# A decoder layer on one core: the expert gating moved into the last attention iteration

## The reference

```python
x = layernorm(x + self_attention(x))          # attends over the 8 entries, rotary by position, 16 heads of 16
x = layernorm(x + cross_attention(x, ctx))    # 375 context rows per entry, 16 heads of 64, gated by tanh
x = layernorm(x + moe(x))
# moe: logits = x @ gate_w (8 experts); the two largest are kept, softmax over the two;
#      sum over the chosen experts of w_e * swiglu(x, w1_e, w2_e, w3_e), hidden width 512,
#      plus a shared swiglu for every token
```

## Time and profile before

| | us |
|---|---|
| median of 3 runs | 819.84 (818.64 to 822.49) |
| the profiled execution | 820.82 |
| its span, first to last instruction | 819.0 |
| PE busy | 658.7 (80%) |
| DVE busy | 540.1 (66%) |
| ACT busy | 411.2 (50%) |
| POOL busy | 218.4 (27%) |

### The profile page before, as it was taken

The page is one execution under the profiler, slowest core; times in us unless marked ns, Lnnn a source line. Parts: engine busy times, 40 slices in busy tenths (PEclk is TensorE's granted clock), DMA queues, the critical chain, the costliest instruction groups (busy, mean ns, idle before and its releaser), DMA issues. The chain is left out here.

```text
span 819.0 us, 13429 instructions
## 1 busy us (share of the span) xinstructions
PE 658.7 (80%) x4168; PEld 527.8 (64%) x4168; DVE 540.1 (66%) x1124; ACT 411.2 (50%) x1021; POOL 218.4 (27%) x223
## 2 busy tenths in 40 slices
PE   5717679899899899889889889988767864789980
PEld 4616468678678687777778777867565452456650
DVE  3974366886886886887786877786747851963332
ACT  2314175584574565476465557554533621853431
POOL 3540031232231222232232133122212530233331
PEclk9865689999998998999998999999956986999995
DMA  9113200200110210210210110040216444533324
GB/s 285 46 40 120 62 1 11 78 26 13 53 49 0 61 51 0 61 51 0 51 61 0 37 50 26 11 128 28 78 52 217 139 143 138 174 60 58 53 33 102
DMA packets 55634, 54.24 MB, mean 66 GB/s; under 512 B 17256, under 2 KB 44976, under 8 KB 55600
## 3 DMA queue, kind: packets, MB, share of 16 engines
q1 hardware_dynamic: 51504, 48.61, 19.7%
q0 software_dynamic: 4096, 5.19, 3.9%
HBM read 43.67 MB, written 10.13 MB: 66 GB/s over the span
## 5 line engine op out<-in xcount | busy, mean ns | idle before, releaser
L582 POOL TENSOR_TENSOR probs<-probs,c_rcp 112x750 f32<-112x750 f32 x64 | 92.0, 1437 | 317.5 <-DVE c_rcp L942 317.5
L705 ACT ACTIVATE probs<-ps_s,c_neg 112x375 f32<-112x375 f32 x128 | 72.3, 575 | 30.3 <-DVE c_neg L934 30.1
L1243 PE MATMUL ps_t<-ident,probs 112*125 112x112 f32 x384 | 56.4, 285 | 21.3 <-DVE cpt_lo L946 21.2
L1243 PEld LDWEIGHTS ps_t<-ident,probs 112*125 112x125 f32 x384 | 50.0, 195 | 29.0 <-issue 24.4
L1543 POOL DMA_INDIRECT moe_sum<-gsh_hi,xs_in x21 | 33.6, 1602 | 106.4 <-DMA moe_sum<-gsh_hi,xs_in 63.6
L932 DVE TENSOR_REDUCE c_max<-ps_s 112x2 f32<-112x750 f32 x64 | 59.8, 934 | 2.2 <-PE ps_s L133 1.3
L613 ACT ACTIVATE kt_hi<-ps_o 128x376 fp32r<-128x376 f32 x64 | 31.4, 491 | 58.3 <-PE ps_o L133 58.3
L131 PE MATMUL ps_o<-cpt_hi,v_lo 125*128 125x224 f32 x192 | 58.1, 303 | 2.0 <-DVE kt_lo L821 1.7
L1863 PE MATMUL ps_h<-w_ex,xst_hi 128*128 (+1 forms) x168 | 58.2, 389 | 1.4 <-DVE xst_lo L1630 0.9
L946 DVE TENSOR_TENSOR cpt_lo<-ps_t,cpt_hi 125x672 fp32r<-125x672 f32 x64 | 54.6, 853 | 6.0 <-ACT cpt_hi L613 5.9
L131 PE MATMUL ps_o<-ctxt_hi,w_k_lo 128*128 128x376 f32 x128 | 49.9, 390 | 10.2 <-DVE oct_lo L821 10.0
(11 more groups left out here) (289 smaller groups left out, 1946.4 us busy)
## 6 DMA issues: line engine op xcount, KB each, us to landing
chunk<-in_L_ffn_ew_dram SPq DMA_DIRECT2D x24, 512.0 KB, 3.5
spare<-in_L_ffn_ew_dram SPq DMA_DIRECT2D x18, 512.0 KB
store<-in_L_ffn_ew_dram SPq DMA_DIRECT2D x6, 512.0 KB, 5.8
ctx_raw<-in_ctx_dram SPq DMA_DIRECT2D x8, 375.0 KB
moe_in<-chunk SPq DMA_DIRECT2D x1, 2709.0 KB, 14.8
xs_in<-moe_in SPq DMA_DIRECT2D x21, 129.0 KB
plain_raw<-in_L_xattn_w_kv_dram SPq DMA_DIRECT2D x2, 1024.0 KB, 15.0
store<-in_L_ffn_sw_dram SPq DMA_DIRECT2D x3, 512.0 KB, 6.5
```

What stands on the lines that cost most here:

```text
L582: pool.tensor_tensor(p, p, r, ALU.mult).then_inc(sg["p_normed"], 1)
L705: act.activation(probs[:, s % 2, h, :], ps_s[0:N, h, 0:SK], ACT.Exp, bias=c_neg[:, s % 2, h:h + 1], scale=CROSS_SCALE, accum_out=c_sum[:, ...
L1243: last = pe.transpose(ps_t[0:SKT, h, t * N:(t + 1) * N], probs[:, s % 2, h, t * SKT:(t + 1) * SKT], ident[0:N, 0:N])
```

## The change

Nothing of what is computed changes but the order in which overflow tiles are given out. The edits:

- **Places in the last iteration.** A function `late` on each engine. PE's entries are in the table `LATE_PE`, which gives (pair, place) to step; on DVE, ACT and POOL `late(s)` stands at the end of pair `s`.
- **What goes there.** Gate weights' scale (pairs 0 to 2), transposes and split of entries 0 to 6 (pairs 0 to 3), the last three chunk maxima (pairs 0 to 2) and the shared weights' three maxima, now from `raw` (pairs 2 and 3), logits and top two of seven entries (pair 4), the weights' scales (pairs 4 and 5), ranking, slots and weights of seven entries (pair 5), `room_left` (pair 6), the conversion of the shared weights (pairs 6, 7 and after the last `o_lo`), constants on POOL (pair 0), 14 of 16 scatters on POOL (three behind pair 6, eleven behind pair 7, ahead of the last `rstd`). ACT copies seven entries into `rows` (pair 4); `copy_rows` goes, the first choice's row is now `x2_all` itself, two columns wider.
- **The eighth entry appended.** In the expert block its transposes come first; its logits follow unit 0, its ranks unit 1; `slots` then places it behind the seven, in a home tile's free rows or a new overflow tile. Two scatters follow.
- **Loads.** `gate_w` and the first set are loaded in the attention block (the set behind the third conversion); SP loads sets 2 and 3, then eight tiles (`TB` is 8 instead of 6) as soon as all scatters have landed, then sets 4 and 5.
- **Scale of the outputs.** The factor `c_y` isn't in the rows any more: POOL multiplies it in for each tile (`weigh`), and `y_copy` waits for that.
- **Memory.** `Slab` puts tensors of the two blocks in the same bytes; the first block's semaphores are cleared and their numbers used again.

```diff
-TB = 6
+TB = 8
-CHUNKS = 3 * (EXP + 1)
-LATE = CHUNKS - 3 * (B - 1)
+CHUNKS = 3 * EXP
+EARLY = B - 1
+LATE_PE = {(0, 2): ["X0"], (1, 0): ["GS1"], (1, 2): ["X1"], (2, 0): ["GS2"], (3, 2): ["X2"], (3, 4): ["X3"], (4, 0): ["SC1"], (4, 2): ["LG"],
+           (5, 0): ["SC2"], (5, 2): ["RK"]}
...
+            sp.wait_ge(ffn_sg["w_lo"], 3)
+            load_weights(sp, raw, *expert_weights(A, 0), ffn_sg["raw_loaded0"])
...
+            def late(s):                                   # POOL
+                if s == 0:
+                    make_constants()
+                elif s == 5:
+                    pool.wait_ge(ffn_sg["gap_ready"], 1)
+                    pool.tensor_tensor(G.gap_e[:, GATED[0]], G.euler[:, GATED[0]], G.gap[:, GATED[0]], ALU.pow)\
+                        .then_inc(ffn_sg["gap_exp"], 1)
+                elif s == 6:
+                    pool.wait_ge(ffn_sg["slots0"], 1)
+                    pool.wait_ge(ffn_sg["weighing0"], 3)
+                    pool.wait_ge(ffn_sg["rows_copied"], 2)
+                    pool.wait_ge(ffn_sg["made"], MADE + 2)
+                    scatter_rows(pool, ffn_sg, G, xs, early[0:3])
+                elif s == 7:
+                    scatter_rows(pool, ffn_sg, G, xs, early[3:])
...
-                    if not more and s >= PAIRS - LATE:
-                        chunk_max(3 * b + s - PAIRS + LATE)
+                    if not more:
+                        late(s)
...
+            def late(s):                                   # DVE
+                if s == 0:
+                    dve.wait_ge(ffn_sg["gw_loaded"], 16)
+                    dve.wait_ge(ffn_sg["made"], MADE)
+                    dve.tensor_reduce(G.m_gate[:, :], gw_raw[:, :, :].rearrange("p k e -> p (k e)"), X, ALU.max,
+                                      apply_absolute_value=True).then_inc(ffn_sg["gate_scaling"], 1)
+                    x2t_lo(0)
+                    chunk_max(3 * EARLY)
+                elif s == 1:
+                    largest_row(...)          # 3 small: column maximum of a transposed row, a floor, the exponent's bits
+                    x2t_lo(1)
+                    chunk_max(3 * EARLY + 1)
+                elif s == 2:
+                    scales_from(...)          # 4 small: the scale and its inverse
+                    chunk_max(3 * EARLY + 2)
+                    shared_max(0)
+                elif s == 3:
+                    dve.wait_ge(ffn_sg["gw_hi"], 1)
+                    lo_part(dve, G.gw[1] ...)
+                    x2t_lo(2)
+                    x2t_lo(3)
+                    shared_max(1)
+                    shared_max(2)
+                    dve.wait_ge(sg["chunk_max"], CHUNKS + 3)
+                    dve.tensor_reduce(G.m_cols[:, :], w_max[:, :].rearrange("p (j i) -> p i j", i=3), X, ALU.max)
+                elif s == 4:
+                    gate_top_two(dve, ffn_sg, G, 0, late_bank("LG"))
+                    largest_row(...)
+                elif s == 5:
+                    slots()
+                    scales_from(...)
+                    gate_weights(dve, ffn_sg, G, 0)
+                elif s == 6:
+                    room_left()               # 9 small
+                    ...                       # c_gate, c_y: 3 small
+                    convert(0)
+                elif s == 7:
+                    convert(1)
...
+            convert(2)
             x2_moments(B - 1)
...
+            def late(f):                                   # PE
+                elif f == "SC1":
+                    pe.wait_ge(ffn_sg["scaling"], 1)
+                    pe.wait_ge(ffn_sg["x2t_lo"], 4)
+                    pe.transpose(late_bank(f)[0:3, 0:P], G.m_cols[:, :], ident[:, :]).then_inc(ffn_sg["scale_full"], 1)
+                elif f == "LG":
+                    gate_logits(pe, ffn_sg, G, 0, late_bank(f))
+                elif f == "RK":
+                    rank_early()
...
-            for j in range(1, 6):
+            for j in (2, 3):
+                load_set(j)
+            for t in range(TB):
+                load_tile(t)
+            for j in (4, 5):
                 load_set(j)
...
             for u in range(UNITS):                         # PE, expert block
                 unit(u)
                 if u == 0:
-                    rank_tokens()
+                    gate_logits(pe, sg, G, 1, ps_logits)
+                if u == 1:
+                    rank_last()
```

More of the change, by code:

```diff
@@ new lines, with batches, three, lo_part @@
+GATED = (slice(0, EARLY), slice(EARLY, B))
+MADE = 13
+def batches(ph):
+    return range(B)[GATED[ph]]
+def three(pe, out, lhs, rhs, start, stop):
+    for n, (a, b) in enumerate(((0, 0), (1, 0), (0, 1))):
+        last = pe.matmul(out, lhs[a], rhs[b], start=start and n == 0, stop=stop and n == 2)
+    return last
+def lo_part(dve, dst, src, scale, part):
+    return dve.scalar_tensor_tensor(dst, src, scale, part, op0=ALU.mult, op1=ALU.subtract)
+def largest_row(dve, sg, tag, full, m_row, inf_row, ps):
+    dve.wait_ge(sg[full], 1)
+    dve.reduce_max(m_row, ps, X).then_inc(sg[tag], 1)
+    dve.wait_ge(sg[tag], 2)
+    dve.tensor_scalar(m_row, m_row, 2.0 ** -100, None, ALU.max).then_inc(sg[tag], 1)
+    dve.wait_ge(sg[tag], 3)
+    dve.tensor_tensor(m_row.bitcast(I32), m_row.bitcast(I32), inf_row.bitcast(I32), ALU.bitwise_and).then_inc(sg[tag], 1)
@@ new lines, in scales_from, with gate_logits @@
+def scales_from(dve, sg, tag, full, p, sc, un, inf_col, ps):
+    dve.wait_ge(sg[full], 2)
+    dve.tensor_copy(p, ps).then_inc(sg[tag], 1)
+    dve.wait_ge(sg[tag], 5)
+    dve.tensor_tensor(sc.bitcast(I32), p.bitcast(I32), inf_col.bitcast(I32), ALU.bitwise_xor).then_inc(sg[tag], 1)
+    dve.tensor_scalar(un, p, 2.0 ** -14 / X_SCALE, None, ALU.mult).then_inc(sg[tag], 1)
+    dve.wait_ge(sg[tag], 7)
+    dve.tensor_scalar(sc, sc, 2.0 ** 13, None, ALU.mult).then_inc(sg[tag], 1)
+def gate_logits(pe, sg, G, ph, ps):
+    pe.wait_ge(sg["x2t_lo"], 4 + ph)
+    pe.wait_ge(sg["gw_lo"], 1)
+    for i, b in enumerate(batches(ph)):
+        for k in range(KD):
+            last = three(pe, ps[0:N, i * EXP:(i + 1) * EXP], [t[:, k, b * N:(b + 1) * N] for t in G.x2t],
+                         [t[:, k, :] for t in G.gw], start=k == 0, stop=k == KD - 1)
+    last.then_inc(sg["logits_full"], 1)
@@ L122, in later, with scatter_rows @@
+def scatter_rows(pool, sg, G, xs, pairs):
+    for b, c in pairs:
+        src = G.x2_all[0:N, b, :] if c == 0 else G.rows[:, b, :]
+        pool.indirect_dma_start(xs[:, :], bass.IndirectOffsetOnAxis(G.slot[:, c, b:b + 1], 0), src, None)\
+            .then_inc(sg["scattered"], 16)
 def later(count):
@@ L1538, in _ @@
+            for t in range(3):
+                weigh(t)
             pool.wait_ge(sg["sums_started"], 32)
```

664 lines of the change are left out of this document (389 added, 275 removed).

## The result

The changed kernel takes 830.3 us (median of 4 runs, 829.5 to 835.7) against 820.4 us before on the same chip: ratio 1.0121, 95% interval 1.0093 to 1.0149. The forecast was 825.0, the range 813 to 832. The sign and the range held; the growth is 9.9 us where 5.2 were forecast.

A forecast was written before the change was run, and what follows sets the result against it. Late attention was taken as bound by a cross-engine loop, the expert block's head by a serial thread and a tile-load wait. Attention +26, head -20.0, tile 0's transposes -0.8: +5.2 us, 825.0 against the median; range 813 to 832.

The forecast's parts named there:

- tail: End of the last attention iteration: the third conversion stands before the last residual, +1.1 us.
- The loop argument: Late attention pairs, from pair 3: VectorE work appended to a pair lengthens it whole, less what TensorE covers; loop 5.55 us.
- rival A: Pairs 4 to 7: VectorE's idle time is real room, attention grows only 12 to 16.5 us, 811 to 816; chance 0.25.
- Pairs 0 to 3 and 7: Last attention iteration, at full clock: +3.3, +2.85, -0.2, +3.05 and, for pair 7, +1.6 us.
- TensorE would wait at `m_cols`: Pair 4: TensorE idles some 4 us before the transpose of `m_cols`, which VectorE makes ready at the end of pair 3.
- The head's gap part: Expert block: the gap from the shared path's end to the tiles' landing goes, -10.1 us; tile 0 at full clock, -2.7.
- the head as a whole: Expert block up to the first accumulating scatter: -20.0 us, bounds -15 and -23, and 0.8 less for tile 0's transposes.
- The scatters are hidden: Eleven scatters before the last `rstd`: 16.2 us in 16.8 of room, 0.6 to spare; 6 to spare or 5 late as bounds.
- the 5 that was the bound: Pairs 6 and 7: conversions on VectorE would hold up GpSimd's scatters, by up to 5 us; 0 was taken.
- VectorE's work, pairs 4 to 6: Added VectorE work in late attention: +1.8, +2.7 and +1.85 us, 6.35 together.
- TensorE's stop, what stands behind it, and the clock, pairs 4 to 6: Late attention: +2.7 us in pair 4, +1.15 in pair 5, +4 for the clock, 7.85 together.
- the clock's part: Pairs 4 to 6: TensorE partly at half clock after idling, +4 us, the middle of 0 and +8.3.

The follow-up runs named there:

- a_order: Changed kernel with the two scale transposes moved behind the K and V products of pairs 4 and 5: 821.3 us, ratio 1.0020.
- b_double: Kernel before with the raw chunk's maximum taken three times in late pairs 2 to 7 (twelve added reductions): 840.1 us, ratio 1.0221.
- b_double_warm: b_double plus extra constant-matrix products in TensorE's gaps in pairs 3 to 7 and the tail: 828.2 us, ratio 1.0106.
- a_const: Changed kernel with VectorE's `m_gate` maximum in pair 0 moved behind `x2t_lo` and the chunk maximum: 829.6 us, ratio 1.0105.
- a_warm: Changed kernel plus extra constant-matrix products in TensorE's gaps in pairs 3 to 7 and the tail: 828.1 us, ratio 1.0091.
- a_order_warm: a_order plus extra constant-matrix products in the gaps of pairs 3, 6, 7 and the tail: 825.7 us, ratio 1.0044.
- a_tiles_late: Changed kernel with tile loads back behind the second store and weight set 6, first three `weigh` steps behind the stores: 840.9 us, ratio 1.0261.
- b_tiles: Kernel before with the first eight tile loads issued once its scatters landed, ahead of the shared expert's stores and weight set 6: 809.3 us, ratio 0.9856.
- a_order_warm_sc6: a_order_warm with six scatters instead of three in pair 6 and eight instead of eleven behind pair 7: 820.6 us, ratio 1.0002.
- a_order_conv: a_order with the shared weights' conversion back at the expert block's start, the first expert's weight load behind it: 820.5 us, ratio 0.9994.

## Why the prediction was half right

Pair by pair, in microseconds of growth over the kernel before, from one `c_max` (from pair 5 on, `cpt_lo`) that opens a pair to the next, pair 7 up to the last `cpt_lo`:

| | predicted, full clock | after | a_order |
|---|---|---|---|
| pair 0 | +3.3 | +3.2 | +3.2 |
| pair 1 | +2.85 | +2.5 | +2.5 |
| pair 2 | -0.2 | +0.6 | +0.6 |
| pair 3 | +3.05 | +2.9 | +3.2 |
| pair 4 | +4.5 | +7.0 | +1.6 |
| pair 5 | +3.85 | +5.95 | +3.6 |
| pair 6 | +1.85 | +2.7 | +2.7 |
| pair 7 | +1.6 | +1.5 | +1.5 |
| tail | +1.1 | +3.3 | +0.4 |
| sum | +21.9 | +29.7 | +19.4 |

**Right.** The loop argument, against the 24 us of idle VectorE that spoke for rival A: b_double and b_double_warm bear it out. Pairs 0 to 3 and 7, each within 0.8. The view that TensorE would wait at `m_cols`: 3.38 us, some 4 forecast. The head's gap part within 2, by two kernels; the head as a whole within 1.2 of 20.8, though with errors that cancel: the second gate came 1.5 us earlier than forecast, the units behind it lost 2.1 more (from the gate at 673.56 to the next at 678.80 it is 5.24 us instead of 3.57, with the granted clock at 0.57 from 673 to 676). The scatters are hidden in this kernel: they end at 644.43 with 4.81 us to spare before the `rstd`.

```profile
643.49 0.94 POOL L291 DMA_INDIRECT moe_in<-rows,slot  x1 [0.30 <-issue]
649.25 0.57 POOL L753 TENSOR_TENSOR rstd<-mv,const_neg_half 112x1 f32<-112x1 f32 x1 [4.81 <-DVE mv L1090]
```

Of the 4.81, 2.95 are ScalarE's late start: in a_const and a_order, without it, 1.89 are left, against 0.6 forecast. The eleven took 13.9 us, 1.25 apart, where the sum had 16.2 at 1.47 (and its bound of 6 to spare left out the 0.3 us between two scatters). The conversions did hold some scatters up: the two that started beside one took 1.32 and 1.44 us instead of 0.94, about 0.9 us in all, not the 5 that was the bound. With pair 7 3 us shorter, in a_warm and a_order_warm, the scatters were 1.0 late.

**The step that failed** is a size and not the mechanism. In the terms of the sum, in microseconds of the profiled run:

| term | predicted | measured |
|---|---|---|
| pairs 0 to 3 and 7 | 10.6 | 10.8 |
| VectorE's work, pairs 4 to 6 | 6.35 | 5.8 |
| TensorE's stop, what stands behind it, and the clock, pairs 4 to 6 | 2.7 + 1.15 + 4 = 7.85 | 9.8 |
| tail | 1.1 | 3.3 |
| head | -20.8 | -19.6 |
| start of the iteration | 0 | +1.1 |
| accumulating scatters | 0 | -1.4 |
| sum | 5.1 (5.2 with attention rounded to 26) | 9.8 |

(VectorE's work is what it does from 602.37 to 605.24, 613.32 to 617.22 and 622.65 to 625.46, less a maximum of 1.25 us each; the third row is the rest of the three pairs' growth.) The third and fourth rows, each some 2 us short, are the terms that were mis-sized most. In the third the clock's part was the middle of 0 and 8.3, +4; against the full-clock sum the three pairs took 5.4 more (2.5, 2.1 and 0.85). The sum let TensorE work at full clock behind its stop: in pair 4 4.8 us from the scale product to the transposes. Measured are 6.9 (592.25 to 599.15), most of it at the half clock that the long stop had kept down. Stop and clock were costed as separate terms, one of them by a coin's middle; they come together. a_order, which has the same work without the stop, takes 5.4 + 2.35 = 7.7 of the 9.8 us away. No run separates the clock's share of that from the stop's over all three pairs: a_warm, which filled the gaps, got 1.05 us back in pair 4 and nothing in pair 5.

**The tail** has +3.3 instead of +1.1, and most of that is a late start of ScalarE in this run. ScalarE's timeline of the changed kernel, and then that of a_const, the same work in the same tail:

```profile
644.68 0.54 ACT L837 ACTIVATE oct_hi<-ps_o 64x112 fp32r<-64x112 f32 x2 [5.18 <-remote]
```
```profile
643.07 0.54 ACT L837 ACTIVATE oct_hi<-ps_o 64x112 fp32r<-64x112 f32 x2 [2.25 <-PE ps_o L306]
```

The `oct_hi` of pair 7 came 5.15 us after `cpt_lo`'s start here, and some 2.2 after it in a_order; its input had been written by 641.7. From the last `cpt_lo` to `x_all` it is 10.33 us in this run, 7.38 in a_const and in a_order, and 8.25 in a_tiles_late. What stopped ScalarE is not known, and the cause stays open; it is in one profiled run only. Without these 2.95 us attention grew by 26.8, against 26 forecast. That also says how far the agreement may be read: the profile's +9.9 us is 3 us of that late start and 1 us of chance in the iteration's start more than the edit explains, and yet the four timed runs have a median of +9.9 as well, while a_const, without the late start and with 0.7 us less in pairs 0 and 1, has +7.7 (8.6 by the ratio). Between 1 and 3 us of the result stay open.

## What to carry to other kernels

In a loop across engines an engine's idle time is latency: ask what the added work stands in front of, and count it whole unless a run says otherwise. A small operation that waits belongs at the very end of an in-order queue's independent work: here the place of two 0.3 us transposes was worth nearly all that the change lost. And before moving computation to free a queue, look whether the transfer alone can be moved: that edit alone gives 11 us here, while the hoisted gating bought 8 us of head for 20 to 30 us of attention.

## What the runs showed that was not expected

- Products that compute nothing made two kernels faster: 2.8 us of 63.5 in attention at b_tiles, 5.55 of 80.4 at b_double.
- TensorE's first transpose of the expert block follows the start of the last `x_all` by 1.5 us in after, a_order and a_order_warm_sc6, and by 5.0 and 5.3 us in a_warm and a_order_warm, where GpSimd's last scatter had ended 0.6 us before that `x_all`; in a_order_conv, with the scatter as late but without the products and the weights' load, by 2.05.
- The same 21 accumulating scatters took 98.4 to 99.0 us from first to last in seven kernels and 100.3 to 102.0 in the other eight. The seven are all six kernels with constant products, though these stand well ahead of the scatters, and a_order_conv, which has none. Whether the products shorten the stretch is therefore open, and so is how; 2 to 3.4 us of what such a kernel gains in time lie there.
